# A deep transformer stage on one core: PE's eight pairs of a layer in line, and new orders for all engines

## The reference

```
for i in range(6):
    x = attn_layer(shift_tokens(x), Wqkv[i], q_scale[i], k_scale[i], Wo[i]) + x
    x = ffn_layer(shift_tokens(x), ln_g[i], ln_b[i], W1[i], b1[i], W2[i], b2[i]) + x

attn_layer:  q, k, v = split(x @ Wqkv);  q, k = l2norm(q) * qs, l2norm(k) * ks
             q, k = rotated by cos/sin tables with a position-dependent scale
             sim = 8 * q k^T inside the token's window of 32 and the one before
             out = softmax(sim) @ v;  return out @ Wo
ffn_layer:   hg = layernorm(x) @ W1 + b1;  a, gate = split(hg)
             return (a * gelu(gate)) @ W2 + b2
```

## Time and profile before

| | us |
|---|---|
| median of 3 runs | 4956.29 (4952.42 to 4957.85) |
| profiled execution | 4950.25 |
| its span | 4948.6 |
| PE busy | 4317.4 (87%) |
| DVE busy | 3975.7 (80%) |
| ACT busy | 3045.9 (62%) |
| POOL busy | 2752.6 (56%) |
| mean granted clock of TensorE | 0.936 of full speed |

### The profile page before, as it was taken

How to read it: one execution, slowest core, us unless ns; L and a number is a source line. 1 busy time by engine, 2 the same in 40 slices (tenths; PEclk the granted TensorE clock), 3 DMA queues, 4 the chain that set the end, 5 groups by cost and what they waited for, 6 DMA issues and landing times. The chain is left out here.

```text
span 4948.6 us, 174542 instructions
## 1 busy us (share of the span) xinstructions
PE 4317.4 (87%) x70208; PEld 3409.7 (69%) x70208; DVE 3975.7 (80%) x6281; ACT 3045.9 (62%) x5515; POOL 2752.6 (56%) x1392
## 2 busy tenths in 40 slices
PE   5797899999589899899998998989989989999985
PEld 4565577777467777777777776777777777777774
DVE  5334799998688889888898888988889888998883
ACT  3365333333257777776777777777777767777763
POOL 0222666666266566665666556655666556666561
PEclk9799899999789999999999999999999999999997
DMA  1233000000132233322333224233233232332232
GB/s 48 93 122 119 1 1 0 0 0 1 35 70 58 65 70 82 83 61 57 85 78 74 64 57 99 64 68 71 57 88 77 64 69 66 81 83 60 60 68 55
DMA packets 239161, 303.67 MB, mean 61 GB/s; under 512 B 93940, under 2 KB 129272, under 8 KB 237944
## 3 DMA queue, kind: packets, MB, share of 16 engines
q1 hardware_dynamic: 223192, 247.08, 21.9%
q0 software_dynamic: 15264, 46.14, 2.9%
HBM read 50.37 MB, written 28.84 MB: 16 GB/s over the span
## 5 line engine op out<-in xcount | busy, mean ns | idle before, releaser
L2100 POOL TENSOR_TENSOR raw<-raw,rs 128x1024 f32<-128x1024 f32 x384 | 792.9, 2065 | 1089.7 <-DVE rs L1937 627.8
L2092 POOL TENSOR_TENSOR spare<-raw,table 128x1024 f32<-128x1024 f32 x384 | 914.9, 2393 | 261.7 <-DVE raw L1916 250.8
L1909 DVE TENSOR_TENSOR raw<-raw,table 128x1024 f32<-128x1024 f32 x384 | 732.2, 1907 | 42.4 <-POOL spare L2092 40.4
L1781 ACT ACTIVATE raw<-shared 128x512 f32<-128x512 f32 x768 | 463.5, 603 | 333.9 <-PE shared L1559 310.9
L1557 PE MATMUL shared<-wqkv_lo,xT_hi 128*128 128x512 f32 x1152 | 567.5, 493 | 33.0 <-DVE xT_lo L1946 25.8
L1903 DVE TENSOR_REDUCE ss<-spare 128x16 f32<-128x1024 f32 x384 | 466.1, 1214 | 155.1 <-ACT spare L1786 154.2
L1916 DVE TENSOR_TENSOR raw<-raw,spare 128x1024 f32<-128x1024 f32 x384 | 550.8, 1434 | 13.2
L1612 PE MATMUL trn<-ident,raw 128*128 128x128 f32 x3072 | 484.0, 280 | 13.5 <-POOL raw L2100 4.0
L1558 PE MATMUL shared<-wqkv_hi,xT_lo 128*128 128x512 f32 x1152 | 474.1, 412 | 0.0
L1559 PE MATMUL shared<-wqkv_hi,xT_hi 128*128 128x512 f32 x1152 | 472.2, 410 | 0.0
L1786 ACT ACTIVATE spare<-shared 128x512 f32<-128x512 f32 x768 | 462.3, 602 | 1.9 <-DVE ss L1903 1.9
(11 more groups left out here) (203 smaller groups left out, 9723.9 us busy)
## 6 DMA issues: line engine op xcount, KB each, us to landing
Vw<-V SPq DMA_DIRECT2D x1344, 128.0 KB
xs<-X SPq DMA_DIRECT2D x144, 128.0 KB, 2.1
Vw<-V SPq DMA_DIRECT2D x192, 64.0 KB
e_plain<-in_L_ffn_W SPq DMA_DIRECT2D x16, 704.0 KB, 4.7
split_hi<-e_high POOLq DMA_DIRECT2D x16, 704.0 KB, 5.9
split_lo<-e_low POOLq DMA_DIRECT2D x16, 704.0 KB, 7.1
wqkv_hi<-split_hi POOLq DMA_DIRECT2D x30, 256.0 KB, 3.1
wqkv_lo<-split_lo POOLq DMA_DIRECT2D x30, 256.0 KB, 3.2
```

Source lines behind the costliest of these rows:

```text
L1909: dve.tensor_tensor(x, x, table[:, part, 0, k][:, None, :].to_broadcast([P, H, HD]), ALU.mult).then_inc(cos_part, 1)
L2092: pool.tensor_tensor(dst, src, by[:, None].to_broadcast([P, H, 2, 32]), ALU.mult).then_inc(sin_part, 1)
L2100: pool.tensor_tensor(x, x, rs[:, at:at + H][:, :, None].to_broadcast([P, H, HD]), ALU.mult).then_inc(rotated, 1)
```

## The change

The step constants of all engines in the deep stage get new values, B_ADD_STEP, B_STAT_STEP, B_POWER_STEP and the orders of slots keep theirs, and PE's program of a layer has its bodies i = 2 to 7 written out by a Python loop instead of a hardware loop over i = 2 to 6 and body 7. The loop over layers stays, and so do all loops of the other engines. With Python numbers for i, PE's waits count from constants and the register of l alone.

```diff
--- before.py
+++ after.py
@@ -1158,39 +1158,39 @@
 BLOCKS = DEPTH * GROUP
 PROJ_ORDER = [(k, part, a) for k in range(2) for part in range(2) for a in range(2)] \
     + [(0, 2, 0), (1, 2, 0), (0, 2, 1), (1, 2, 1)]
-PROJ_STEPS = (-15, -14, -13, -12, -11, -10, -9, -8, -5, 7, 11, 12, 15)
+PROJ_STEPS = (-15, -13, -12, -11, -10, -9, -8, -6, -5, 4, 5, 10, 15)
 TURN_ORDER = [(0, 0, 0), (0, 1, 0), (1, 0, 0), (1, 1, 0), (0, 0, 1), (0, 1, 1), (1, 0, 1), (1, 1, 1)]
-TURN_STEPS = (4, 6, 7, 8, 9, 13, 14, 15)
+TURN_STEPS = (7, 9, 10, 11, 12, 13, 14, 15)
 TURNED_FOR = (4, 8)
 STEPS = 16
-SINE_STEPS = (-10, -9, -4, 3)
-REDUCE_STEPS = (-9, -8, -7, -3)
-COSINE_STEPS = (-5, -4, 2, 7)
-NEWTON_STEP = -2
-SCALE_STEPS = (-2, 1, 3, 5)
-SCORE_STEPS = (0, 5)
-HIGHEST_STEPS = (4, 10)
-EXP_STEPS = (5, 12)
-TOTAL_STEPS = (9, 15)
-NORM_STEPS = (8, 16)
-FLIP_STEPS = (11, 18)
-MIX_STEPS = (13, 21)
-DRAIN_STEPS = (15, 22)
-OUT_STEPS = (25, 26)
-ADD_ATTN_STEP = 28
+SINE_STEPS = (-11, -9, -7, 1)
+REDUCE_STEPS = (-13, -8, -7, -4)
+COSINE_STEPS = (-5, -1, 2, 7)
+NEWTON_STEP = -3
+SCALE_STEPS = (-3, -2, 4, 7)
+SCORE_STEPS = (0, 8)
+HIGHEST_STEPS = (6, 12)
+EXP_STEPS = (7, 12)
+TOTAL_STEPS = (8, 15)
+NORM_STEPS = (10, 15)
+FLIP_STEPS = (17, 21)
+MIX_STEPS = (18, 24)
+DRAIN_STEPS = (21, 25)
+OUT_STEPS = (28, 29)
+ADD_ATTN_STEP = 31
 B_STAT_STEP = 0
 B_POWER_STEP = 1
-B_AWAY_STEP = 7
-B_NORMAL_STEP = 8
-B_TURN_STEP = 13
-B_AFFINE_STEP = 13
-B_LOW_STEP = 14
-B_HIDDEN_STEPS = (17, 20, 24)
-B_GELU_STEPS = (17, 20, 24)
-B_GATED_STEPS = (17, 23, 27)
-B_OUT_STEP = 28
+B_AWAY_STEP = 2
+B_NORMAL_STEP = 6
+B_TURN_STEP = 10
+B_AFFINE_STEP = 11
+B_LOW_STEP = 12
+B_HIDDEN_STEPS = (15, 22, 24)
+B_GELU_STEPS = (15, 22, 24)
+B_GATED_STEPS = (16, 22, 25)
+B_OUT_STEP = 29
 B_ADD_STEP = 31
-CHUNK_STEPS = (22, 23, 24, 29, 45, 47)
+CHUNK_STEPS = (22, 24, 24, 26, 37, 46)
 ROWS = 16
 
 
@@ -1750,14 +1750,12 @@
             body(Pair(0, 0))
             body(Pair(0, 1))
             with pe.Fori(0, DEPTH - 1) as l:
-                with pe.Fori(2, GROUP - 1) as i:
+                for i in range(2, GROUP):
                     body(Pair(l, i))
-                body(Pair(l, GROUP - 1))
                 body(Pair(l + 1, 0))
                 body(Pair(l + 1, 1))
-            with pe.Fori(2, GROUP - 1) as i:
+            for i in range(2, GROUP):
                 body(Pair(DEPTH - 1, i))
-            body(Pair(DEPTH - 1, GROUP - 1))
             body(Pair(DEPTH, 0))
             body(Pair(DEPTH, 1))
```

## The result

The changed kernel takes 5170.4 us (median; 5157.7 to 5184.1), against 4957.1 before beside it: a ratio of 1.0432, 95% interval 1.0397 to 1.0468. It is 213 us slower. I had forecast 4712, faster, with 0.04 on slower.

What follows compares the result with a forecast made beforehand. PE, busy 87%, bounded the kernel, DVE nearly as full. 47 bodies at 67.6 us plus 22 for outer jumps made 3199 against 3443: -244 (110 and 134), 4706, with 6.0 to the median 4712 us; range 4615 to 4850.

Steps and rivals of the forecast that it cites:

- part 2: New step orders in the deep stage: consumers stand further behind producers, PE's waits shrink; 134 us gain, 2.9 a body.
- 2.0 us a step: PE's work in one step of a deep-stage body, taken as 64.0/32, used to size the added cover.
- Part 1: PE's inner loop goes: 24 of 28 jumps at 3.31 us, 79 us, and 30 from the clock; -110, range -79 to -130.
- Rival 4: PE's 3.3 us belong to code that is passed, not to the jump; only the orders gain: 4822 us, chance 0.03.
- code in line costs nothing: PE's longer code, 11 to 19 bodies in the program, executes as many instructions; instruction fetch costed at nothing.
- gaps of 3 us elsewhere in PE's line: Sign against the inner loop's removal: L1622's issue gaps should fall from 28 to 4; wrong if such gaps appear elsewhere.
- DVE as the next bound: In the deep stage's bodies DVE is late next: 65.4 us in a clean body, 67.6 on average with its waits.
- The other signs: Deep stage: clock 0.98 or more, average body 66 to 69.5 us, DVE busy 63 to 66 with few waits.
- Rival 3: Slower: DVE's cosine and add held by POOL's work, 2.1 us more for each; 5065 us at half held, chance 0.04.
- Rival 1: Orders bring nothing: PE's wait for POOL's E becomes one for DVE; 4846 us (4826 to 4877), chance 0.20.
- Rival 2: PE alone bounds, DVE fits beneath it; a body is 64.0 + 0.6 us, 4571 us in all, chance 0.14.

Runs made afterwards that it cites:

- v_twice: The changed kernel with the first half of V there twice, by the parity of the sequence; orders and code in line unchanged: 4861.3 us, 0.9816 to the kernel before.
- line_old_orders: The kernel before with PE's pairs written in line alone, the orders of before kept: 4857.7 us, 0.9813 to the kernel before.
- loop_new_orders: The changed kernel with PE's inner loop as before, so the new orders alone: 5174.9 us, 1.0458 to the kernel before.

## Why the prediction was wrong

**The step that failed** is in part 2: "what changes is how far a consumer stands behind its producer". The prediction then goes through flips, hidden products, x, maximum, chunks and the shift of a block, but not v, whose first slot moves from step 7 to 4 of a half body while the last one stays at step 15. With SP it looked only at the order of its queue, and not at what its moves must leave free: V. ACT's wait for the emptying of V was in the code of before, and the sum put it at nothing. Measured are 294.3 us of it in 90 places, 3.27 each, and 309 us between this kernel and `v_twice`. None of the rivals was this one; the slower one named DVE and POOL, and its 0.04 was the price of the omission.

The wait could have been found beforehand, but the prediction's 2.0 us a step would not have sized it. From the tight place shown above it gives 3 x 2.0 less 2.7 = 3.3 us, twice in 47 bodies, 310 us, which is right by luck: it leaves out that the moves land 1.5 us after their last issue, and it takes a place that few others are like. With the median slack of 9.1 us the same sum gives no wait at all. The traces show why. From a sequence's last v drain to ACT's arrival at the next one's first the median was 21.2 us before and is 11.0 after: the three steps took away 10 us and not 6, since steps are not equally long. The 16 moves need 12.3 us (median after) and the landing.

**Part 1 was right**: -110 forecast, within -79 to -130; -93 alone. The 24 gaps went, 79 us, and the clock rose from 0.95 to 0.97. That the sum came out near is in part luck: PE's busy time fell by 58 us (3117 to 3060 in the 47 bodies) where 30 were taken for the clock, and longer waits for POOL's E (22 us), before hidden products (some 13) and for the E that DVE takes from sco (11) took back some 45 of the 137. But the parts do not add: with ACT's wait in place the same edit gives little or nothing. That a jump costs PE 3.3 us was right as well. The Trainium skill (Advanced Engine Details and Errata, Control Flow Timing) has about 108 ns for a compare-and-branch. The 3.3 us that PE loses here are something else, as the instruction packets show: at each of the 28 jumps of the kernel before, PE falls idle, the packet starts 0.4 to 0.7 us later, takes 1.0 us (median), and PE goes on 1.6 to 2.0 us after its landing. Rival 4 is dead with it, and with the 4 places that are left of 28.

**That code in line costs nothing was right, but the code of the new orders does cost.** The gaps inside PE's runs come to 98 us in line and 112 us with the loops, against 6 us in `line_old_orders`, so they are the price of the orders. The prediction had no term for them, though it named the sign: gaps of 3 us elsewhere in PE's line, and here they go up to 4.0 us. The Trainium skill (Runtime: NRT & Kernel Launch, Instruction fetch mechanics) calls the cost of crossing from one block of code to the next "mostly hidden". The gaps of up to 3.5 us in `v_twice` say that in dense stretches of this kernel it is not.

**The rest of part 2** was forecast at -134. Free of V's wait (`v_twice` against `line_old_orders`) it is 0: 4861 and 4858. The flip's 145 us for POOL and the 67 us before the first hidden product did go, as forecast; 109 us of gaps and 126 us for ACT's drains (kT, spare, prT, qT) came in their place. **DVE as the next bound was wrong**: without V's wait it is busy 63.6 us of a body's 71.6, and PE waits for it only 24 us in all. What PE waits for there is its own code and ACT, the engine with 62% busy time that the prediction never priced. ACT's queue is where x, flips, turns and v meet; that its order is what matters is argued from these rows, and no run tried another order in it. The other signs failed with V's wait in place: an average body of 78.1 us where 66 to 69.5 was the limit, and a clock of 0.93 where 0.98 was expected.

**Rival 3's mechanism** did not grow. DVE's cosine and add take 1.50 and 1.71 us on average, against 1.91 and 1.43: 8 x 0.28 + 8 x 0.49 = 6.2 us a body over what they take alone, less than the 7.2 before:

```profile
L1914 DVE TENSOR_TENSOR raw<-raw,spare 128x1024 f32<-128x1024 f32 x384 | 657.0, 1711 | 13.2
...
L1907 DVE TENSOR_TENSOR raw<-raw,table 128x1024 f32<-128x1024 f32 x384 | 574.5, 1496 | 3.2 <-issue 0.2
```

**Rival 1** (the orders bring nothing, 4846) is the nearest in time to the kernel without V's wait, but not in its mechanism: what was a wait for POOL's E became gaps and waits for ACT, not for DVE. Rival 2 (PE alone bounds, 4571) was not reached by any kernel.

## What to carry to other kernels

When a producer is moved earlier, ask two questions of its buffer: who fills it, and who must have emptied it. The second wait is as real as the first, and it has no row in the old trace while there is slack. To price it, take from the trace the length of the emptying up to its landing and the spread of the slack over all bodies, not one place, and the time between the two places in the code that are brought together, not a mean step.
Price the two parts of a change apart and together; the gain of one can vanish behind the wait that the other brings. And look at every engine whose queue holds the consumer, also one that is far from the busiest: here it was ACT, at 62%.

## What the runs showed of the hardware

- A jump back at the end of a PE body cost 3.1 to 3.9 us (before and `loop_new_orders`); in the kernel before 0.4 to 0.7 of them pass until the packet of instructions starts and 1.6 to 2.0 after it has landed. The inner loops of DVE, ACT and POOL showed nothing of the kind; at the outer loop's jumps of before they stood 2.5 to 3.6, 2.8 to 3.1 and 1.4 to 2.2 us.
- From the first issue to the last, sixteen moves of V on SP's queue took 10.3 to 13.7 us (medians 11.6 before, 12.3 after), about 0.6 us for the shortest issues; ACT was let go 1.4 us after the last issue at the earliest.
- PE stood idle 0.3 to 4.0 us inside runs of small matmuls, and went on 1.2 to 1.7 us after a packet of instructions had landed (`v_twice`, 73 gaps of over 0.5 us). Moving a mix by two steps cut these gaps from 109 to 8 us, smaller transfers beside them to 67.
